# DLRM tower with pairwise kernels: a quarter of the doubles turned, summed on ScalarE, with other rings for the stages

## What is computed

```python
e = jnp.stack([tbl_f[ids[:, f]] for f in range(32)], axis=1)      # (2048, 32, 64), cut short here
z = jnp.sum(e, axis=-1)                                           # (2048, 32)
outer = jnp.einsum('bpd,pde,bpe->bp', e[:, II], kernels, e[:, JJ])  # (2048, 496)
h = jnp.concatenate([z, outer, dense_ctx], axis=1)                # (2048, 544)
h = jnp.maximum(h @ W_top1 + b_top1, 0.0)                         # 512 wide
h = jnp.maximum(h @ W_top2 + b_top2, 0.0)                         # 256 wide
y = h @ W_top3                                                    # (2048, 1)
```

## Time and profile before

| what | value |
|---|---|
| median of 3 runs | 1012.58 us (1011.55 to 1014.28) |
| profiled execution, its own time | 1018.13 us |
| its span, first to last instruction | 1016.3 us |
| granted TensorE clock, mean | 0.963 |
| HBM read | 27.40 MB |
| instructions | 11896 |

### The profile page before, as it was taken

One profiled execution on the slowest core, in us unless ns is written; L12 is line 12 of the kernel. 1 busy time (PEld: TensorE's weight loads), 2 busy tenths in 40 slices (PEclk: granted clock), 3 DMA queues, 4 the chain that ended last, 5 costly groups with the idle time before them and its releaser, 6 DMA issues.

```text
span 1016.3 us, 11896 instructions
## 1 busy us (share of the span) xinstructions
PE 886.5 (87%) x4608; PEld 311.6 (31%) x4608; DVE 641.3 (63%) x579; ACT 69.3 (7%) x113; POOL 483.6 (48%) x518
## 2 busy tenths in 40 slices
PE   0323579699999999998999999998999999999998
PEld 0111123223333333333333333323333333333333
DVE  0102257578887575687877656676787657688850
ACT  0000000000000001000000101000000101000001
POOL 5774735536565444555666444554556445400000
PEclk9956779999999999999999999999999999999999
DMA  9310101101111000110111010011101000000000
GB/s 348 107 27 15 27 14 19 21 12 23 23 21 23 17 17 18 20 21 20 22 23 22 15 19 17 19 22 19 21 19 24 15 17 19 19 1 1 1 1 0
DMA packets 19777, 28.20 MB, mean 28 GB/s; under 512 B 8901, under 2 KB 9413, under 8 KB 18825
## 3 DMA queue, kind: packets, MB, share of 16 engines
q0 software_dynamic: 16384, 16.81, 8.6%
q1 hardware_dynamic: 3336, 10.63, 2.9%
HBM read 27.40 MB, written 0.01 MB: 27 GB/s over the span
## 4 chain that ended last, share of the span: by engine, by line
PE 77%; another core or an unknown queue 8%; issue 7%; DVE 4%; DMA 2%; ACT 1%; SPq 1%; POOL 1%; DVEq 0%; POOLq 0%
PE m_ps L386 39%; PE acc L398 21%; PE tr L341 4%; DVE prod L300 3%; PE tr L328 3%; PE tr L347 2%; PE m_ps L387 2%; DMA w_sb<-in_w 2%; PE m_ps L341 1%; PE tr L339 1%; PE m_ps L347 1%; PE tr L353 1%; POOL gathered L176 1%; SPq L186 1%
## 5 line engine op out<-in xcount | busy, mean ns | idle before, releaser
L300 DVE TENSOR_TENSOR prod<-m_ps,x_t 128x1024 f32<-128x1024 f32 x512 | 604.3, 1219 | 302.5 <-PE m_ps L387 180.7
L176 POOL DMA_INDIRECT gathered<-in_tbl,idx x512 | 482.9, 943 | 403.4 <-DVE prod L300 178.2
L386 PE MATMUL m_ps<-x_t,k_sb 64*128 64x512 f32 x1024 | 501.4, 623 | 74.6 <-DVE prod L300 35.6
L387 PE MATMUL m_ps<-x_t,k_sb 64*128 64x512 f32 x1024 | 502.3, 624 | 0.0
L386 PEld LDWEIGHTS m_ps<-x_t,k_sb 64*128 64x128 f32 x1024 | 180.7, 191 | 346.9 <-issue 261.6
L398 PE MATMUL acc<-prod,sel 128*32 128x512 f32 x2048 | 247.0, 600 | 0.0
L387 PEld LDWEIGHTS m_ps<-x_t,k_sb 64*128 64x128 f32 x1024 | 180.6, 191 | 0.0
L398 PEld LDWEIGHTS acc<-prod,sel 128*32 128x32 f32 x2048 | 53.7, 109 | 176.5 <-issue 119.6
L328 PE MATMUL tr<-ident,gathered 128*128 128x128 f32 x256 | 44.5, 299 | 50.6 <-DMA gathered<-in_tbl,idx 41.4
L213 ACT ACTIVATE x_t<-tr 128x512 f32<-128x512 f32 x64 | 38.2, 597 | 471.7 <-PE tr L328 275.3
L287 DVE TENSOR_REDUCE z_nat<-gathered 128x8 f32<-128x512 f32 x64 | 43.1, 675 | 38.1 <-DMA gathered<-in_tbl,idx 38.1
(11 more groups left out here) (24 smaller groups left out, 39.6 us busy)
## 6 DMA issues: line engine op xcount, KB each, us to landing
gathered<-in_tbl,idx POOLq DMA_INDIRECT x512
k_sb<-in_kmat SPq DMA_DIRECT2D x7, 1024.0 KB, 14.3
w_sb<-in_w SPq DMA_DIRECT2D x1, 1280.0 KB
k_sb<-in_kmat SPq DMA_DIRECT2D x2, 256.0 KB, 4.2
k_sb<-in_kmat SPq DMA_DIRECT2D x1, 512.0 KB, 6.4
w_sb<-in_w SPq DMA_DIRECT2D x1, 512.0 KB
idx<-in_ids SPq DMA_DIRECT2D x1, 256.0 KB, 2.7
z_sb<-in_dense_t SPq DMA_DIRECT2D x4, 32.0 KB
```

Source lines behind the costliest of these rows:

```text
L176: nc.gpsimd.indirect_dma_start(out=gathered[:, G % GR, t, f, :], out_offset=None, in_=tables[2 * (STAGES - 1 - a) + f], in_offset=bass.Ind ...
L300: nc.vector.tensor_tensor(prod[:, p % PR, :, :], m_ps[:, p % MR, :, :], other, ALU.mult).then_inc(prod_ready, 1)
L386: nc.tensor.matmul(m_ps[:, p % MR, 0, :], k_sb[0:D, d, :], x_t[0:D, q % 2, a0, :], start=True, stop=True)
L387: nc.tensor.matmul(m_ps[:, p % MR, 1, :], k_sb[D:P, d, :], x_t[D:P, q % 2, a1, :], start=True, stop=True).then_inc(unit_done, 1)
```

## The change

A quarter of the doubles, 32 of 128 a pass, is "turned". A turned unit has one tile of 128 samples in the weights (a half of a stage of `x_t`, 64 rows by 128 samples) and the kernels of four stages as the moving operand (64 x 512 out of `k_sb`). The result has samples in the partitions and 4 stages x 128 columns in the row, for each of the two tables of stage m. VectorE multiplies it by the rows as they were gathered. The sum over 64 columns then runs along the row: ScalarE does it with 16 copies of 128x64 in place, each with `accum_out` into one column of `z_turned`. At the end of a pass the 4 tiles of `z_turned` are transposed through `tr` ("t") and become one block of `z_sb`. Eight combinations (block of four stages, m), by 4 tiles, make NT = 32 turned units. The even doubles are ND = 96, in NG = 24 groups and NB = 3 blocks; with ZTURNED and ZSHORT there are again 5 blocks for layer 1.

Work is ordered by step now (NS = 128 a pass: 96 even, 32 turned, the turned ones after even doubles 16 to 91). `AHEAD` replaces `BEFORE` and `AFTER`. The ring of gathered stages grows from 4 to GR = 12, since a turned product reads four stages of rows. `x_t` shrinks from two passes of 16 stages to a ring of XR = 20. The turned products have a ring of BR = 2. ScalarE takes the sums of a turned step SUM_BEHIND = 2 steps later in its queue. At the end, the part of layer 1 that needs neither the last block nor the turned sums comes before them.

```diff
-GR = 4
+GR = 12
+XR = 20
+BR = 2
+COLS = 4
+TURNED = [(1, 0), (1, 1), (1, 2), (2, 0), (2, 1), (2, 2), (3, 10), (3, 11)]
+NT = len(TURNED) * TILES
-    DOUBLES += [(_a, _a, _m, _m) for _m in range(_a)]
+    DOUBLES += [(_a, _a, _m, _m) for _m in range(_a) if (_a // COLS, _m) not in TURNED]
+TURNED_AFTER = [16 + 49 * _i // 20 for _i in range(NT)]
+STEPS = []
+for _d in range(ND):
+    STEPS.append(("even", _d))
+    STEPS += [("turned", _i) for _i, _at in enumerate(TURNED_AFTER) if _at == _d]
-    return 18 + 32 * (q - 1) + 2 * a
+    return NS * (q - 1) + 82 + 8 * a
 for _a in range(STAGES):
+    _s = STEP_OF["even", FIRST[_a]] - 2
+    AHEAD.setdefault((0, max(0, min(_s, 81 - 2 * (STAGES - 1 - _a))) if _a > 1 else 0), []).append(("x", 0, _a))
 for _q in range(1, NQ):
+    AHEAD.setdefault((_q, 6), []).append(("t", _q - 1, 0))
+        AHEAD.setdefault((_q, 14 + 8 * _n), []).append(("h1", _q - 1, _n))
+        AHEAD.setdefault((_q, 46 + 8 * _n), []).append(("h2", _q - 1, _n))
+    AHEAD.setdefault((_q, 62), []).append(("y", _q - 1, 0))
+SUM_BEHIND = 2
-        x_t = sb("x_t", [P, 2, STAGES, QB])
-        gathered = sb("gathered", [P, GR, TILES, 2, D])
+        x_t = sb("x_t", [P, XR, QB])
+        gathered = sb("gathered", [P, TILES, GR, 2 * D])
+        turned = sb("turned", [P, BR, 2, QB])
+        z_turned = sb("z_turned", [P, TILES, P])
 # GpSimd
+                    old_q, old_block = (G - GR) // STAGES, (G - GR) % STAGES // COLS
+                    if old_block:
+                        pool.wait_ge(prod_ready, old_q * NS + LAST_TURNED[old_block] + 1)
-                        pool.wait_ge(prod_ready, GROUP * (group_of_stage(q, a) - 3) + n)
+                        pool.wait_ge(prod_ready, step_of_stage(q, a) - 24 + n)
 # ScalarE
+                if G >= XR:
+                    old_q, old_a = divmod(G - XR, STAGES)
+                    act.wait_ge(prod_ready, old_q * NS + LAST_USE[old_a] + 1)
+            def sum_turned(q, i):
+                c, t = divmod(i, TILES)
+                p, o = q * NS + STEP_OF["turned", i], (q * NT + i) % BR
+                act.wait_ge(prod_ready, p + 1)
+                for n in range(2 * 2 * COLS):
+                    f, u = divmod(n, 2 * COLS)
+                    row = turned[:, o, f, u * D:(u + 1) * D]
+                    last = nc.scalar.activation(row, row, ACT.Copy, accum_out=z_turned[:, t, 16 * c + n:16 * c + n + 1])
+                last.then_inc(turned_summed, 1)
 # VectorE
+            def turned_product(q, i):
+                c, t = divmod(i, TILES)
+                p, r, block = q * NS + STEP_OF["turned", i], q * NT + i, TURNED[c][0]
+                if t == 0:
+                    for landed in gather_landed:
+                        dve.wait_ge(landed, (q * STAGES + COLS * (block + 1)) * GATHERS // IN_FLIGHT * 16)
+                dve.wait_ge(unit_done, p + 1)
+                if r >= BR:
+                    dve.wait_ge(turned_summed, r - BR + 1)
+                at = (q * STAGES + COLS * block) % GR
+                other = gathered[:, t, at:at + COLS, :].rearrange("p c n -> p (c n)").unsqueeze(1).to_broadcast([P, 2, QB])
+                nc.vector.tensor_tensor(turned[:, r % BR, :, :], m_ps[:, p % MR, :, :], other, ALU.mult).then_inc(prod_ready, 1)
 # TensorE
+            def turned_sums(q):
+                pe.wait_ge(turned_summed, (q + 1) * NT)
+                for t in range(TILES):
+                    last = nc.tensor.transpose(tr[:, t * P:(t + 1) * P], z_turned[:, t, :], ident[:])
+                last.then_inc(tr_filled, 1)
+            def multiply_turned(q, i):
+                c, t = divmod(i, TILES)
+                p, at, m = q * NS + STEP_OF["turned", i], K_AT["turned", c], TURNED[c][1]
+                if t == 0:
+                    pe.wait_ge(tr_kept, place("x", q, m))
+                pe.wait_ge(prod_ready, p - MR + 1)
+                for f in range(2):
+                    last = nc.tensor.matmul(m_ps[:, p % MR, f, :], x_t[f * D:(f + 1) * D, (q * STAGES + m) % XR, t * P:(t + 1) * P],
+                                            k_sb[f * D:(f + 1) * D, at:at + COLS, :].rearrange("p c n -> p (c n)"),
+                                            start=True, stop=True)
+                last.then_inc(unit_done, 1)
 # TensorE, at the end
+            pe.wait_ge(prod_ready, NQ * NS)
+            for n in range(H1 // P):
+                layer1_begin(n, m_ps[:, n // 2, n % 2, :])
+            fill("t", LAST, 0)
+            pe.wait_ge(tr_kept, place("t", LAST, 0))
             pe.wait_ge(z_kept, NQ * NB)
             for n in range(H1 // P):
-                layer1(n, m_ps[:, n // 2, n % 2, :], h1_summed)
+                layer1_end(n, m_ps[:, n // 2, n % 2, :], h1_summed)
```

## The result

Timed beside the kernel before on the same chip, the changed kernel took 1092.11 us (median of 4, 1089.22 to 1094.43) against 1013.43 us (1011.55 to 1015.83). The ratio is 1.0774, with a 95% interval from 1.0734 to 1.0813. The forecast was 980 us, in a range up to 1040, and faster: both missed. The profiled execution took 1090.3 us, of which 1088.1 are its span.

What follows compares the result with a forecast made beforehand. PE was taken as the bound, DVE close behind, except in the first 150 us. Three passes gave -30 us, pass 0 -5, tail +1: -34 from 1018.1, so 980 us on the median's scale, range 940 to 1040.

Steps and rivals of the forecast that it cites:

- Steps 1 to 4: Per pass: reduces -15.8 us, turned sums' transposes +0.9, DVE and PE stalling each other +3, ScalarE's small summing copies +2.
- Rival A: ScalarE's summing copies become the bound: 1020 us at 0.32 us a copy, about 1090 at 0.36; chance 0.18.
- Hidden: ScalarE's sums at 0.24 us a copy fit the turned units' period, 4.4 of 4.8 us.
- Rival B: Start of pass 0: late waits not from POOL's runs, ring of 12 removes halts, about 949 us; chance 0.15.
- Step 5, first half: Pass 0's start: one unbroken gather run until about 165 us, 20 products at 168 us, pass 0 -5 us.
- the bad end: Slow bound for pass 0: only 15 products at 168 us, pace staying 1.52 us, ending at 340, +16 us.
- Step 5, second half: Passes 1 to 3: gathers wait for a block's last turned product, at worst 7 steps late of 24; no cost.
- Rival C: POOL never at rest without tower, 1 to 2 us of late waits a stage: 1012 to about 1030 us; chance 0.10.
- Rival A's far end: ScalarE's summing copies at 0.36 us each exceed their period by 112 us in all, total about 1090 us.

Runs made afterwards that it cites:

- the ring alone: Changed kernel's rings and step order, no turned units, all 128 doubles even: 932.84 us (before 933.65); in another session 1061.94 us (before 1017.94).
- the held kernel with half the gathers: Changed kernel, pass 0 gathers held to four stages, one of two gathers per step in passes 1 to 3: 980.37 us (before 1017.94), elsewhere 902.06 (before 933.84).

## Why the prediction was wrong

**Steps 1 to 4, the prices.** In prompt sessions they come out: -10.6 us in passes 1 and 2 and -9.1 in pass 3, where the steps gave -15.8 + 0.9 + 3 + 2 = -9.9 each, and -31.7 us of span in all (900.4 against 932.1) where the sum was -34. (One slip in it: a group's 5.48 us less 3.44 for the doubles leaves 2.04, not 1.97, for the reduce, 0.6 us over 8 groups.) In the late condition pass 3, with gathers in its first half only, still shows -7.1. The copy with its sum was priced at 0.24 us and is 0.24: two instructions, 241 and 188 ns, that lie over each other. The Trainium skill, page "VectorE: DVE Perf Modes", section "The TRN2 errata", gives 240 ns for the first by an estimate, and the trace agrees; that the readout adds nothing to the distance of two, only the timeline tells. Rival A is out: ScalarE is 52% busy, DVE isn't waiting for its sums. "Hidden" held in passes 1 and 2, and in pass 0 it was wrong by 4 to 7 us, perhaps because a stage's copy stands behind sums there while the pace is set by the stages coming in; that reason isn't shown. What the sums cost in the late condition isn't known, since the kernel without them met no late session. Rival B's condition, no late waits at the start, was met in prompt sessions only, and even there the ring was worth 11 us (pass 0 of the ring alone 207.3 against 218.3), not 31, and nearly all of that was given back: 3.1 to 3.3 us in each of passes 1 to 3.

**Step 5, first half: the long run.** This term had the right mechanism and was far too small: -5 us forecast for pass 0, +60.5 measured, of which the ring alone makes 44.8. I let the others crawl at one product per 6 us and set 20 at 168 us; there were 8. The failed step is that I took one rate for a run of any length. The windows of the products (L300) of the kernel before, run, halt, run and halt:

```profile
40.00:88.00 48.00, 6.12 (x5) 0.68 0.14 26
88.00:102.00 14.00, 5.45 (x5) 0.63 0.03 7
102.00:128.50 26.50, 6.09 (x6) 0.74 0.14 27
128.50:143.00 14.50, 7.17 (x7) 0.65 0.02 5
```

Inside the runs 11 products in 74.5 us, one per 6.8; half of the ten that I counted from 90 to 130 us had fallen in the halt. Already that gives 17 at 168 us, not 20. The larger part is that the waits grow as the run goes on. From product to product the changed kernel took 9, 4, 10, 11, 22, 45 and 32 us, and the ring alone 11, 10, 11, 11, 22, 34 and 32. The rows by window hid it, but the timeline of the kernel before had the sign in its first run, where the steps from product to product are 2, 3, 8 and 23 us, and 11 at its end:

```profile
79.78 1.23 DVE L300 TENSOR_TENSOR prod<-m_ps,x_t 128x1024 f32<-128x1024 f32 x1 [21.28 <-remote]
```

The longest unbroken run of the kernel before was 59 us, and I stretched it to 140 without letting the rate fall. The bound is where it should have shown: I put 15 products at the bad end, which the halts had allowed, where a standstill was as open. Six products by 168 us, and 122 at 1.52 us behind them, end pass 0 at 353 us, +29. The ring alone ended it at 367.3 even so, with 8 products at 168: after the run another 9 us passed before the next product (at 176.7 us), and the 120 from there on came every 1.59 us. The other 15.7 us of pass 0 come with the turned units, and they lie behind the run: the first 64 steps are the same with and without turned units (222.8 and 222.5 us), the other 64 take 116.7 against 101.3. They belong to the loss of the next step.

**Step 5, second half: "nothing waits there".** The gathers of a block wait for the block's last turned product, at worst 7 steps late of 24. That no engine waits for those gathers is right, but POOL itself waits, 28 times and 90.1 us in all, 11.1 us at the longest. It then issues what it owes, 13 or 14 gathers without a pause, and in the late condition the others fall behind during it. The 16 steps with that run take 36.0 us, against 21.6 for the same steps in a prompt session; the other 48 steps of the half take 81.4 against 66.1, and the 64 before them 116.8 against 115.8. So half of the pass's 30.7 us lies in the catch-up and half beside it. That this run is the cause of the first half is read from the windows and not isolated by a kernel of its own. For the other half, the held kernel with half the gathers shows that it goes when the gathers thin out (the same 48 steps take 67.4 us), and the ring alone that it isn't there without turned units. The explanation would be slack: with turned units PE is 99.9% busy in a prompt pass 1 (203.34 of 203.5 us), DVE 78%, and a unit crosses three engines instead of two, so a late answer finds nothing that absorbs it. That is argued, not shown. Nor is it parted from another reading: at the prompt pace 16 steps of this half take 21.6 to 22.2 us with turned units and some 23.1 without, and their 16 gathers at 1.25 us fill 20 of them, so that a faster kernel leaves POOL less rest.

**Rival C** was this mechanism: POOL seldom at rest, 1 to 2 us of late waits a stage. It had chance 0.10, with +16 for the start and 25 to 50 us over the stages. By these terms it comes to 980 + 21 + 25 to 50, 1026 to 1051 us; the 1012 and 1030 that stand in the prediction are added up wrong. Measured against the forecast it is +65.5 in pass 0 and +21, +17 and +3 in passes 1 to 3; so its size for the stages was right and the start was far too small. Rival A's far end, about 1090, is the time that was measured, but by chance: its cause, a copy of 0.36 us, isn't there.

**The mechanism as a whole.** The kernel before takes 80 us more in the late condition (1013 against 933). I had seen that loss at the start and named its sign, and then treated it as nearly a constant that the change would leave alone, though the change touches just what it hangs on: how long POOL gathers without rest.

**What stays open.** What decides between the two conditions isn't known. Of the sessions, 4 were prompt and 3 late, besides the one of the result. It isn't fixed by the chip: the last two sessions bear the same chip's number, and one was prompt and the other late. Within a session it held for every kernel. What holds the answers up wasn't found either: the profile calls it remote. And the late results of the experiments are single runs.

## What to carry to other kernels

A wait that "nobody waits for" still has to be followed for one more step: what the engine does when it is released, here a burst of DMAs, and what that burst does to the others. Where a trace shows that some activity holds the other engines up, count what they do inside its unbroken stretches alone, see whether the change lengthens these (a deeper ring takes away halts in which others caught up), and let the bad bound be a standstill. And time a kernel in more than one session: this change is 3.4% faster in one condition of the chip and 7.7% slower in the other, and neither number alone says what it is worth.

## What the runs showed of the hardware

- Under GpSimd's indirect DMAs of 128 rows, one every 1.25 us, DVE stood up to 43 us and ScalarE up to 73 us (85 with the ring alone) in a wait that nothing recorded on the core ended, and ScalarE instructions without a wait started up to 1.2 us late, in some sessions. In others the same program ran 144 of them in one run with no late answer, and the kernel before took 933 instead of 1013 to 1035 us.
- The gathers themselves weren't slower: one every 1.25 us in both. With a gather for every second step in place of each, the kernel before was at its prompt times (214.0 us a pass) even in a late session.
- In a late session, rests of 1.9 us behind every four gathers, filled with memsets, gave 47 products by 168 us where unrested gathers left 8; a gap of 0.1 us behind each gather gave nothing.
- ScalarE's copy with a sum put out is two instructions (241 and 188 ns for 128x64) that overlap; one such pair starts every 0.24 us.
